# An expert's down projection in five products instead of six: features split 128 and 48, the 48 stacked as high and low parts

## The chip, the cores and the metric

One core of a Trainium2 chip runs the whole program. TensorE (PE) multiplies, VectorE (DVE) and ScalarE (ACT) do the elementwise work and move results out of PSUM, GpSimd (POOL) does some elementwise work and issues the indirect transfers, SyncE (SP) issues most of the others. The metric is the device time of one execution in microseconds (us).

## The reference, cut to what matters

The reference is one transformer block with modulation (adaLN): attention over 8 sequences of 256 tokens with 256 features, then a feed-forward part with one shared expert and 8 routed experts, two of which each token uses. Float32 inputs and outputs. The change touches only the routed experts:

```python
B, S, H, F, FS, N = (2, 128, 256, 176, 352, N_EXPERTS)      # here 2048 tokens, F = 176
g = jnp.einsum('th,nfh->ntf', h, gate_w)
u = jnp.einsum('th,nfh->ntf', h, up_w)
e = jnp.einsum('ntf,nhf->nth', jax.nn.silu(g) * u, down_w)   # the down projection: 176 -> 256
routed = jnp.einsum('nth,tn->th', e, wmat)
```

## The kernel before, in words

All products run on TensorE in the type `fp32r`, and each value is split into a high part (its rounding to that type) and a low part (the rest). `mm3` makes one product of three: low times high, high times low, high times high, lines 343, 344 and 345. Each matmul instruction is recorded with its weight load (PEld, LDWEIGHTS), of the stationary operand.

Attention, the shared expert and the routing run first, for 8 sequences interleaved by hand; the order on each engine is written out in the program, and engines meet at semaphores. The tokens are then scattered to a buffer sorted by expert, padded for each expert to tiles of 128 rows, and 39 tiles follow (`NT`). This is the routed stage. In step t the engines do, each in this order:

- TensorE: `pe_tile_up` of tile t+1 (six products with 352 moving columns: gate and up together), `pe_tile_act` of tile t (two transposes, line 1375, of the activated values `av` from rows to columns), `pe_tile_in` of tile t+3 (two transposes, line 1353), `pe_tile_down` of tile t-1 (six products with 256 moving columns).
- ScalarE: silu (line 1392), the high part of the activated values (`act_tile_act`, line 1396), the high part of the input (line 1388), the result of the down projection from PSUM to `yo` (line 1402).
- VectorE: silu times up (line 1430), the low part of the activated values (`dve_tile_lo`, line 1436), the low part of the input (line 1406), every fourth step four small operations on the routing data (lines 1419 to 1424), and in late steps one of the final additions (lines 1490 to 1502).
- GpSimd: the scatter of the finished rows (line 1441). SyncE: the loads of the tiles to come.

The down projection sums over 176 features. Before, they are cut into two halves of 88 (`FH`), both on partitions 0 to 87: two transposes of 88 columns, and two times three products with 88 rows each.

The weights of expert e come by two transfers (`sp_weights`) to one of two staging buffers `wstage`, ScalarE rounds them to the high part (`act_weights`), GpSimd or VectorE makes the low part (`split_weights`). Experts 0 and 1 are fetched at the start of the program, the others during attention, each when its buffer is free.

Of the kernel before, what the change touches and what calls it, by code (L numbers as in the profile page):

```python
# [8 lines left out]
ALU = mybir.AluOpType  # L9
ACT = mybir.ActivationFunctionType  # L10
F32 = mybir.dt.float32
# [5 lines left out]
ds = bass.ds  # L17

P = 128
# [9 lines left out]
def adaln_block(nc, x_in, w_qkv, b_cols, w_proj, b_proj, gate_col, cam_w0, cam_w1,  # L29
                router_t, gu_t, down_t, sh_gu_t, sh_down_t, c_t, w_mod, out):  # L30
    B, S, D = x_in.shape
    NE = router_t.shape[1]
    F = down_t.shape[1]
    FS = sh_down_t.shape[0]
    KD = D // P
# [3 lines left out]
    NT = (2 * T + NE * (P - 1)) // P  # L39
    REGION = T + P  # L40
    ROW = D + META
    FH = F // 2
    FT = [(f, min(P, FS - f)) for f in range(0, FS, P)]
    UNR = 3
    assert D == KD * P == 256 and S == TT * P == 256 and NT % UNR == 0 and F <= 256

    with ExitStack() as ctx:
        def sb(name, shape, dt=F32):
# [289 lines left out]
        def parts(t, *idx):  # L338
            return t[0][idx], t[1][idx]

        def mm3(pe, out_ap, l, r, start, stop):

            pe.matmul(out_ap, l[1], r[0], start=start, stop=False)  # L343
            pe.matmul(out_ap, l[0], r[1], start=False, stop=False)  # L344
            return pe.matmul(out_ap, l[0], r[0], start=False, stop=stop)  # L345
# [417 lines left out]
        if True:  # L763
# [71 lines left out]
            def sp_gate(sp, q):  # L835
                sp.dma_start(gring[q % 4][:], modrow[q:q + 1, 4 * D:5 * D].to_broadcast([P, D]).unsqueeze(1)).then_inc(gb_sems[q % 4], 16)

            def pool_setup(pool):
                pool.memset(minus_half[:], -0.5).then_inc(s_const, 1)
                pool.memset(eps_t[:], EPS).then_inc(s_const, 1)  # L840
                pool.memset(ident[:], 0.0).then_inc(s_const, 1)
                pool.memset(before[:], 0.0).then_inc(s_const, 1)
                pool.wait_ge(s_const, 4)
                pool.affine_select(out=ident[:], in_=ident[:], compare_op=ALU.not_equal, fill=1.0,
                                   base=0, pattern=[[-1, P]], channel_multiplier=1).then_inc(s_ident_ready, 1)

                pool.affine_select(out=before[:], in_=before[:], compare_op=ALU.is_ge, fill=1.0,
                                   base=0, pattern=[[-1, P]], channel_multiplier=1).then_inc(s_const, 1)
                pool.memset(ones[:], 1.0).then_inc(s_const, 1)
                pool.memset(ramp[:], 1.0).then_inc(s_const, 1)  # L850
                pool.iota(ebase[:], pattern=[[0, NB], [REGION // P, NE]], base=0, channel_multiplier=0,
                          allow_small_or_imprecise_dtypes=True).then_inc(s_const, 1)
                pool.wait_ge(s_const, 7)
                pool.affine_select(out=ramp[:], in_=ramp[:], compare_op=ALU.is_ge, fill=0.0,
                                   base=-NE, pattern=[[-NE, NR]], channel_multiplier=1).then_inc(s_const, 1)
                pool.iota(token_id[:], pattern=[[P, B * TT]], base=0, channel_multiplier=1,
                          allow_small_or_imprecise_dtypes=True).then_inc(s_const, 1)
                pool.iota(eidx[:], pattern=[[1, NE]], base=0, channel_multiplier=0,
                          allow_small_or_imprecise_dtypes=True).then_inc(s_const, 1)
                pool.iota(tidx[:], pattern=[[1, NT]], base=1, channel_multiplier=0,  # L860
                          allow_small_or_imprecise_dtypes=True).then_inc(s_const, 1)
                pool.iota(erow[:], pattern=[[REGION, NE]], base=0, channel_multiplier=0,
                          allow_small_or_imprecise_dtypes=True).then_inc(s_const, 1)
                for i, at, step in ((0, 0, 1), (1, 1, 1), (2, 0, REGION // P)):
                    pool.iota(pcols[:, i:i + 1], pattern=[[1, 1]], base=at, channel_multiplier=step,
                              allow_small_or_imprecise_dtypes=True).then_inc(s_const, 1)
                pool.memset(within[:, 0:1], 0.0).then_inc(s_const, 1)
                pool.wait_ge(s_const, 10 + 7)
# [370 lines left out]
            def pool_rstd1(pool, first, after):  # L1239
                at = slice(2 * TT * first, 2 * TT * after)  # L1240
                pool_rstd(pool, s_var1, after, mv1[:, at, 1], rs1[:, at], s_rstd1, 2 * first)
# [33 lines left out]
                sp.dma_start(mh[u][:], modrow[b:b + 1, 2 * D:4 * D].to_broadcast([P, 2 * D]).rearrange("p (j d) -> p j d", d=D)).then_inc((s_mh0_in, s_mh1_in)[u], 16)  # L1275

            eT = [tuple(h[:, 0, q * S:(q + 1) * S].rearrange("p (k n) -> p k n", k=KD) for h in h2T) for q in range(4)]
            avT = [tuple(h[0:FH, 1, q * S:(q + 1) * S].rearrange("p (k n) -> p k n", k=2) for h in h2T) for q in range(2)]

            sg = [wstage[q][:, 0:F] for q in range(2)]  # L1280
            av = [wstage[q][:, F:2 * F] for q in range(2)]
# [4 lines left out]
            xt_in = [h2all[:, r, :] for r in range(8)]  # L1286
            pad = exchange[:, 4 * ROW:5 * ROW]

            def expert(e, part, at, n):
                base = (0, W1, 2 * W1, 2 * W1 + W2)[part]  # L1290
                return experts_w[0:(P if part < 2 else FH), ds(e * WE + (base + at), n)]

            def bank2(t, n=256):
                return t[:, 0:2 * n].rearrange("p (a n) -> p a n", a=2)
# [4 lines left out]
            def sp_weights(sp, e, r):  # L1299

                if e >= 2:
                    sp.wait_ge((s_split_even, s_split_odd)[r], e // 2)
                sp.dma_start(wstage[r][:, 0:W1].rearrange("p (k n) -> p k n", k=KD),
                             gu_t[:, ds(e, 1), :].rearrange("(k p) o n -> p k (o n)", p=P)).then_inc((s_est0_in, s_est1_in)[r], 16)
                sp.dma_start(wstage[r][0:FH, W1:].rearrange("p (j n) -> p j n", j=2),
                             down_t[ds(e, 1)].rearrange("o (j p) n -> p (o j) n", p=FH)).then_inc((s_est0_in, s_est1_in)[r], 16)

            def act_weights(act, e):
                r = e % 2
                act.wait_ge((s_est0_in, s_est1_in)[r], 16 * (e - r) + 32)  # L1310
                if e == 0:
                    act.wait_ge(s_wlo_later, 2 + NF)
                    act.wait_ge(s_wlo, 3)
                    act.wait_ge(s_modrow_out, 16)
                    act.wait_ge(s_bvp_done, 1)
                elif e == NE // 2:
                    act.wait_ge(s_qk_done, 2 * B)
                elif e > NE // 2:
                    act.wait_ge(*((s_v_done, B), (s_v_done, B), (s_s2_done, B))[e - NE // 2 - 1])
                act.activation(expert(e, 0, 0, W1), wstage[r][:, 0:W1], ACT.Copy)  # L1320
                act.activation(expert(e, 2, 0, W2), wstage[r][0:FH, W1:], ACT.Copy).then_inc(s_ew_hi, 1)

            def split_weights(eng, e):
                r = e % 2
                eng.wait_ge(s_ew_hi, e + 1)
                eng.tensor_tensor(expert(e, 1, 0, W1), wstage[r][:, 0:W1], expert(e, 0, 0, W1).bitcast(F32), ALU.subtract)
                eng.tensor_tensor(expert(e, 3, 0, W2), wstage[r][0:FH, W1:], expert(e, 2, 0, W2).bitcast(F32),
                                  ALU.subtract).then_inc((s_split_even, s_split_odd)[r], 1)


# [40 lines left out]

            def pe_tile_act(pe, t, r):
                pe.wait_ge(s_ea_ready, t + 1)
                for j in range(2):
                    last = pe.transpose(ATb[r % 2][0:FH, j * P:(j + 1) * P], av[r % 2][:, j * FH:(j + 1) * FH], ident[:])  # L1375
                last.then_inc(s_eat_done, 1)

            def pe_tile_down(pe, experts, t, r):
                e = expert_of(pe, experts, r)
                pe.wait_ge(s_ea_lo, t + 1)  # L1380
                for j in range(2):
                    last = mm3(pe, EDN[r % 2][:, 0:D], parts(avT[r % 2], slice(None), j),
                               (expert(e, 2, j * D, D), expert(e, 3, j * D, D)), j == 0, j == 1)
                last.then_inc(s_edn_done, 1)

            def act_tile_in(act, t, r):
                act.wait_ge(s_ext_done, t + 1)
# [5 lines left out]

            def act_tile_act(act, t, r):
                act.wait_ge(s_eat_done, t + 1)
                act.activation(avT[r % 2][0], bank2(ATb[r % 2], P)[0:FH], ACT.Copy).then_inc(s_ea_hi, 1)

            def act_tile_out(act, t, r):
                act.wait_ge(s_edn_done, t + 1)
# [33 lines left out]
            def dve_tile_lo(dve, t, r):  # L1433
                q = r % 2
                dve.wait_ge(s_ea_hi, t + 1)
                dve.tensor_tensor(avT[q][1], bank2(ATb[q], P)[0:FH], avT[q][0].bitcast(F32), ALU.subtract).then_inc(s_ea_lo, 1)

            def pool_tile(pool, t):
                pool.wait_ge(s_emeta, META_OPS * (t // 4 + 1))
# [66 lines left out]
            with nc.Block() as block:  # L1506
# [68 lines left out]
                @block.gpsimd  # L1575
                def _(pool):
                    pool_setup(pool)
                    pool_rstd1(pool, 0, 1)
                    pool_rstd1(pool, 1, 2)
                    pool_rstd1(pool, 2, 4)  # L1580
# [675 lines left out]
```

## Time and profile before

| | |
|---|---|
| median of 3 runs | 291.94 us (290.74 to 292.01) |
| the profiled execution | 291.79 us, its span from the first to the last instruction 290.0 us |
| granted TensorE clock, mean | 0.976 of full speed |
| PE busy | 257.4 us, 89% of the span |
| DVE busy | 190.3 us, 66% |
| ACT busy | 161.2 us, 56% |
| POOL busy | 128.4 us, 44% |

The span is what the profile covers; the 1.8 us around it belong to the execution and not to any instruction. A busy share is an average over stages with different limits. A matmul's duration in the records is its way through the array, longer than the distance to the next one: what a stream of them costs is read from the distances between their starts.

### The profile page before, as it was taken

Reading aid. Unit: us, or ns where it says so; the run is one execution under the profiler, and the core shown is the slowest. Engines: PE = TensorE matmul, PEld = TensorE weight load, DVE = VectorE, ACT = ScalarE, POOL = GpSimd, SP = SyncE. Lnnn points to the kernel's source line nnn. Section 1 sums busy time; section 2 is a strip of 40 time slices with the busy share of each in tenths; the row PEclk is TensorE's granted clock in tenths of the full one; section 3 lists DMA queues with packets and bytes.
Section 4 is the critical chain, followed back from the end, with each engine's and each line's share of the span. In section 5 each row is a group of like instructions: output and inputs, shape, how many; then the busy total and the mean of one; then the engine's idle time right before and its main releaser. Section 6 shows DMA issues by size and latency. Waiting matters only on the chain.

```text
span 290.0 us, 6198 instructions
## 1 busy us (share of the span) xinstructions
PE 257.4 (89%) x1820; PEld 237.6 (82%) x1820; DVE 190.3 (66%) x579; ACT 161.2 (56%) x429; POOL 128.4 (44%) x146
## 2 busy tenths in 40 slices
PE   0899999898999999999999689999999999999900
PEld 0797688897889989888899579989999999999700
DVE  1675875139988581883697864745555467868893
ACT  2438568878467564747354554446566565656500
POOL 3120404654181078848972855203444454544630
PEclk9999999999999999999999999999999999999955
DMA  7894015341442013142320225344334485584464
GB/s 237 278 347 95 0 32 194 111 122 66 109 112 74 3 57 122 45 126 76 79 108 11 84 92 180 107 125 146 113 129 129 132 254 162 183 251 149 132 189 141
DMA packets 29319, 36.98 MB, mean 128 GB/s; under 512 B 4468, under 2 KB 23903, under 8 KB 29288
## 3 DMA queue, kind: packets, MB, share of 16 engines
q1 hardware_dynamic: 24056, 27.19, 32.3%
q0 software_dynamic: 3408, 8.46, 7.8%
q10 hardware_dynamic: 1824, 0.94, 1.1%
q8 instruction: 16, 0.26, 0.4%
q14 instruction: 15, 0.12, 0.2%
HBM read 24.78 MB, written 12.71 MB: 129 GB/s over the span
## 4 chain that ended last, share of the span: by engine, by line
PE 75%; DVE 7%; issue 5%; ACT 4%; DMA 3%; POOL 3%; ACTq 1%; SPq 0%; DVEq 0%; POOLq 0%
PE bank L343 17%; PE bank L345 17%; PE bank L344 16%; PE bank L1138 4%; PE bank L1353 3%; PE bank L1375 3%; PE bank L1110 3%; PE bank L1130 2%; PE bank L1093 2%; PE bank L1121 2%; PE bank L1102 2%; PE bank L1011 1%; DMA mh<-routed_out 1%; PE bank L540 1%; DMA routed_in<-h2all,slot_u 1%
## 5 line engine op out<-in xcount | busy, mean ns | idle before, releaser
L1441 POOL DMA_INDIRECT routed_out<-yo_all,dest x39 | 40.1, 1028 | 54.8 <-ACT yo_all L1402 35.5
L343 PE MATMUL bank<-experts_w,h2T_lo 128*128 (+1 forms) x156 | 50.6, 325 | 0.1
L345 PE MATMUL bank<-experts_w,h2T_hi 128*128 (+1 forms) x156 | 47.2, 303 | 0.0
L344 PE MATMUL bank<-experts_w,h2T_hi 128*128 (+1 forms) x156 | 47.0, 301 | 0.0
L706 POOL DMA_INDIRECT routed_in<-h2all,slot_u x32 | 31.5, 986 | 23.5 <-DVE slot_u L687 13.3
L1430 DVE SCALAR_TENSOR_TENSOR wstage<-wstage,wt,bank 128x176 f32<-128x176 f32 x39 | 15.5, 397 | 27.9 <-ACT wstage L1392 27.9
L343 PEld LDWEIGHTS bank<-experts_w,h2T_lo 128*128 128x128 f32 (+1 forms) x156 | 29.6, 190 | 0.5 <-issue 0.5
L344 PEld LDWEIGHTS bank<-experts_w,h2T_hi 128*128 128x128 f32 (+1 forms) x156 | 29.7, 190 | 0.0
L345 PEld LDWEIGHTS bank<-experts_w,h2T_hi 128*128 128x128 f32 (+1 forms) x156 | 29.4, 188 | 0.0
L343 PE MATMUL bank<-h2T_hi,wsgu_lo 128*128 128x256 f32 (+1 forms) x96 | 27.9, 290 | 1.5 <-issue 1.5
L345 PE MATMUL bank<-h2T_hi,wsgu_hi 128*128 128x256 f32 (+1 forms) x96 | 27.1, 282 | 1.1 <-issue 1.1
L344 PE MATMUL bank<-h2T_lo,wsgu_hi 128*128 128x256 f32 (+1 forms) x96 | 27.0, 281 | 0.0
L1392 ACT ACTIVATE wstage<-bank 128x176 f32<-128x176 f32 x39 | 12.4, 318 | 22.1 <-PE bank L345 22.1
L343 PE MATMUL bank<-hT_hi,wqk_lo 128*128 128x256 f32 x64 | 20.2, 316 | 2.0 <-DVE hT_lo L1223 2.0
L1402 ACT ACTIVATE yo_all<-bank 128x256 f32<-128x256 f32 x39 | 15.0, 385 | 11.8 <-PE bank L345 6.3
L1147 ACT ACTIVATE exchange<-bank,nm 128x256 f32<-128x256 f32 x32 | 14.8, 472 | 7.7 <-DVE nm L1208 6.1
L344 PE MATMUL bank<-hT_lo,wqk_hi 128*128 128x256 f32 x64 | 19.0, 297 | 0.0
L345 PE MATMUL bank<-hT_hi,wqk_hi 128*128 128x256 f32 x64 | 19.0, 297 | 0.0
L343 PEld LDWEIGHTS bank<-h2T_hi,wsgu_lo 128*128 128x128 f32 (+1 forms) x96 | 17.3, 180 | 2.0 <-issue 1.7
L345 PEld LDWEIGHTS bank<-h2T_hi,wsgu_hi 128*128 128x128 f32 (+1 forms) x96 | 17.3, 180 | 1.2 <-issue 1.2
L344 PEld LDWEIGHTS bank<-h2T_lo,wsgu_hi 128*128 128x128 f32 (+1 forms) x96 | 17.3, 180 | 0.1
L1208 DVE TENSOR_REDUCE nm<-bank 128x2 f32<-128x512 f32 x16 | 11.0, 689 | 8.7 <-PE bank L1093 5.4
(248 smaller groups left out, 760.6 us busy)
## 6 DMA issues: line engine op xcount, KB each, us to landing
h2all<-routed_in SPq DMA_DIRECT2D x39, 130.0 KB, 2.2
wstage<-gu_t SPq DMA_DIRECT2D x8, 352.0 KB
res<-x SPq DMA_DIRECT2D x4, 512.0 KB, 9.0
mx<-modrow SPq DMA_DIRECT2D x8, 256.0 KB, 3.7
mh<-modrow SPq DMA_DIRECT2D x8, 256.0 KB
exchange<-routed_out SPq DMA_DIRECT2D x8, 256.0 KB
wmod_s<-w_mod SPq DMA_DIRECT2D x3, 512.0 KB, 9.7
wstage<-down_t SPq DMA_DIRECT2D x8, 176.0 KB
```

The lines of the kernel that those rows point to most:

```text
L343: pe.matmul(out_ap, l[1], r[0], start=start, stop=False)
L344: pe.matmul(out_ap, l[0], r[1], start=False, stop=False)
L345: return pe.matmul(out_ap, l[0], r[0], start=False, stop=stop)
L706: pool.indirect_dma_start(out=routed_in, out_offset=bass.IndirectOffsetOnAxis(slot_u[:, i, j:j + 1], 0), in_=h2all[:, j % (2 * NB), :], in ...
L1110: last = pe.matmul(Sb[u][:, t * S:(t + 1) * S], th[u][:, t * P:(t + 1) * P], KL[u][:], start=False, stop=(t == TT - 1), skip_group_check=True)
L1138: last = pe.matmul(TR[u][:, t * D:(t + 1) * D], PT[u][:, k, t * P:(t + 1) * P], VV[u][:, k, P:P + D], start=(k == 0), stop=(k == TT - 1))
L1147: last = act.activation(pr[u][:, t, :], Sb[u][:, t * S:(t + 1) * S], ACT.Exp, bias=nm[u][:, i, t:t + 1], accum_out=ls[u][:, i, t:t + 1])
L1208: dve.tensor_reduce(nm[u][:, int(second), :], bank(Sb[u]), AX.X, ALU.max, negate=True).then_inc(s_max2 if second else s_max1, 1)
L1392: act.activation(sg[r % 2], EGU[r % 2][:, 0:F], ACT.Silu).then_inc(s_esilu, 1)
L1402: act.activation(yo[t % 6], EDN[r % 2][:, 0:D], ACT.Copy).then_inc(s_ey_ready, 1)
L1430: dve.scalar_tensor_tensor(av[q], sg[q], wt[:, t % 8:t % 8 + 1], EGU[q][:, F:2 * F], ALU.mult, ALU.mult).then_inc(s_ea_ready, 1)
L1441: pool.indirect_dma_start(out=routed_out, out_offset=bass.IndirectOffsetOnAxis(dest[:, t % 16:t % 16 + 1], 0), in_=yo[t % 6], in_offset=No ...
```

## The change

The 176 features of a tile are cut into 128 and 48 instead of 88 and 88. The first 128 take three products with 128 rows. The other 48 are handled in a block of 64 rows (`HALF`), features 112 to 175, in which the first 16 rows (`GAP`) meet zero weights. ScalarE copies the whole bank (its rows 64 to 127 of the second half hold nothing of use), and VectorE writes the low part of these 64 rows over partitions 64 to 127 of the high tile. The high weights of the 48 features are staged twice, in rows 16 to 63 and 80 to 127. Then one product of 128 rows gives high times high and low times high together, and one of 64 rows gives high times low: five in all. The second transpose has 64 columns of `av` instead of 88, the first 128. The staging buffers get two zeroed regions (`pool_stage_rows`), three transfers for the down weights of an expert instead of one, and the low part of a tile takes two VectorE instructions instead of one.

```diff
@@ -39,10 +39,12 @@
     NT = (2 * T + NE * (P - 1)) // P
     REGION = T + P
     ROW = D + META
-    FH = F // 2
+    HALF = P // 2
+    FB = F - P
+    GAP = HALF - FB
     FT = [(f, min(P, FS - f)) for f in range(0, FS, P)]
     UNR = 3
-    assert D == KD * P == 256 and S == TT * P == 256 and NT % UNR == 0 and F <= 256
+    assert D == KD * P == 256 and S == TT * P == 256 and NT % UNR == 0 and 0 < FB <= HALF
 
     with ExitStack() as ctx:
         def sb(name, shape, dt=F32):
@@ -835,6 +837,10 @@
             def sp_gate(sp, q):
                 sp.dma_start(gring[q % 4][:], modrow[q:q + 1, 4 * D:5 * D].to_broadcast([P, D]).unsqueeze(1)).then_inc(gb_sems[q % 4], 16)
 
+            def pool_stage_rows(pool):
+                for r in range(2):
+                    pool.memset(wstage[r][:, W1 + D:], 0.0).then_inc(s_const, 1)
+
             def pool_setup(pool):
                 pool.memset(minus_half[:], -0.5).then_inc(s_const, 1)
                 pool.memset(eps_t[:], EPS).then_inc(s_const, 1)
@@ -1275,7 +1281,7 @@
                 sp.dma_start(mh[u][:], modrow[b:b + 1, 2 * D:4 * D].to_broadcast([P, 2 * D]).rearrange("p (j d) -> p j d", d=D)).then_inc((s_mh0_in, s_mh1_in)[u], 16)
 
             eT = [tuple(h[:, 0, q * S:(q + 1) * S].rearrange("p (k n) -> p k n", k=KD) for h in h2T) for q in range(4)]
-            avT = [tuple(h[0:FH, 1, q * S:(q + 1) * S].rearrange("p (k n) -> p k n", k=2) for h in h2T) for q in range(2)]
+            avT = [tuple(h[:, 1, q * S:(q + 1) * S].rearrange("p (k n) -> p k n", k=2) for h in h2T) for q in range(2)]
 
             sg = [wstage[q][:, 0:F] for q in range(2)]
             av = [wstage[q][:, F:2 * F] for q in range(2)]
@@ -1286,9 +1292,9 @@
             xt_in = [h2all[:, r, :] for r in range(8)]
             pad = exchange[:, 4 * ROW:5 * ROW]
 
-            def expert(e, part, at, n):
+            def expert(e, part, at, n, rows=P):
                 base = (0, W1, 2 * W1, 2 * W1 + W2)[part]
-                return experts_w[0:(P if part < 2 else FH), ds(e * WE + (base + at), n)]
+                return experts_w[0:rows, ds(e * WE + (base + at), n)]
 
             def bank2(t, n=256):
                 return t[:, 0:2 * n].rearrange("p (a n) -> p a n", a=2)
@@ -1302,12 +1308,16 @@
                     sp.wait_ge((s_split_even, s_split_odd)[r], e // 2)
                 sp.dma_start(wstage[r][:, 0:W1].rearrange("p (k n) -> p k n", k=KD),
                              gu_t[:, ds(e, 1), :].rearrange("(k p) o n -> p k (o n)", p=P)).then_inc((s_est0_in, s_est1_in)[r], 16)
-                sp.dma_start(wstage[r][0:FH, W1:].rearrange("p (j n) -> p j n", j=2),
-                             down_t[ds(e, 1)].rearrange("o (j p) n -> p (o j) n", p=FH)).then_inc((s_est0_in, s_est1_in)[r], 16)
+                if e < 2:
+                    sp.wait_ge(s_const, 18 + e)
+                down = down_t[ds(e, 1)].rearrange("o f n -> f (o n)")
+                for to, of in ((wstage[r][:, W1:W1 + D], down[0:P]), (wstage[r][GAP:HALF, W1 + D:], down[P:F]),
+                               (wstage[r][HALF + GAP:P, W1 + D:], down[P:F])):
+                    sp.dma_start(to, of).then_inc((s_est0_in, s_est1_in)[r], 16)
 
             def act_weights(act, e):
                 r = e % 2
-                act.wait_ge((s_est0_in, s_est1_in)[r], 16 * (e - r) + 32)
+                act.wait_ge((s_est0_in, s_est1_in)[r], 64 * (e // 2 + 1))
                 if e == 0:
                     act.wait_ge(s_wlo_later, 2 + NF)
                     act.wait_ge(s_wlo, 3)
@@ -1318,13 +1328,13 @@
                 elif e > NE // 2:
                     act.wait_ge(*((s_v_done, B), (s_v_done, B), (s_s2_done, B))[e - NE // 2 - 1])
                 act.activation(expert(e, 0, 0, W1), wstage[r][:, 0:W1], ACT.Copy)
-                act.activation(expert(e, 2, 0, W2), wstage[r][0:FH, W1:], ACT.Copy).then_inc(s_ew_hi, 1)
+                act.activation(expert(e, 2, 0, W2), wstage[r][:, W1:], ACT.Copy).then_inc(s_ew_hi, 1)
 
             def split_weights(eng, e):
                 r = e % 2
                 eng.wait_ge(s_ew_hi, e + 1)
                 eng.tensor_tensor(expert(e, 1, 0, W1), wstage[r][:, 0:W1], expert(e, 0, 0, W1).bitcast(F32), ALU.subtract)
-                eng.tensor_tensor(expert(e, 3, 0, W2), wstage[r][0:FH, W1:], expert(e, 2, 0, W2).bitcast(F32),
+                eng.tensor_tensor(expert(e, 3, 0, W2), wstage[r][:, W1:], expert(e, 2, 0, W2).bitcast(F32),
                                   ALU.subtract).then_inc((s_split_even, s_split_odd)[r], 1)
 
 
@@ -1371,17 +1381,17 @@
 
             def pe_tile_act(pe, t, r):
                 pe.wait_ge(s_ea_ready, t + 1)
-                for j in range(2):
-                    last = pe.transpose(ATb[r % 2][0:FH, j * P:(j + 1) * P], av[r % 2][:, j * FH:(j + 1) * FH], ident[:])
+                pe.transpose(ATb[r % 2][:, 0:P], av[r % 2][:, 0:P], ident[:])
+                last = pe.transpose(ATb[r % 2][0:HALF, P:2 * P], av[r % 2][:, F - HALF:F], ident[:])
                 last.then_inc(s_eat_done, 1)
 
             def pe_tile_down(pe, experts, t, r):
                 e = expert_of(pe, experts, r)
                 pe.wait_ge(s_ea_lo, t + 1)
-                for j in range(2):
-                    last = mm3(pe, EDN[r % 2][:, 0:D], parts(avT[r % 2], slice(None), j),
-                               (expert(e, 2, j * D, D), expert(e, 3, j * D, D)), j == 0, j == 1)
-                last.then_inc(s_edn_done, 1)
+                to, (hi, lo) = EDN[r % 2][:, 0:D], avT[r % 2]
+                mm3(pe, to, (hi[:, 0], lo[:, 0]), (expert(e, 2, 0, D), expert(e, 3, 0, D)), True, False)
+                pe.matmul(to, hi[0:HALF, 1], expert(e, 3, D, D, HALF), start=False, stop=False)
+                pe.matmul(to, hi[:, 1], expert(e, 2, D, D), start=False, stop=True).then_inc(s_edn_done, 1)
 
             def act_tile_in(act, t, r):
                 act.wait_ge(s_ext_done, t + 1)
@@ -1393,7 +1403,7 @@
 
             def act_tile_act(act, t, r):
                 act.wait_ge(s_eat_done, t + 1)
-                act.activation(avT[r % 2][0], bank2(ATb[r % 2], P)[0:FH], ACT.Copy).then_inc(s_ea_hi, 1)
+                act.activation(avT[r % 2][0], bank2(ATb[r % 2], P), ACT.Copy).then_inc(s_ea_hi, 1)
 
             def act_tile_out(act, t, r):
                 act.wait_ge(s_edn_done, t + 1)
@@ -1433,7 +1443,9 @@
             def dve_tile_lo(dve, t, r):
                 q = r % 2
                 dve.wait_ge(s_ea_hi, t + 1)
-                dve.tensor_tensor(avT[q][1], bank2(ATb[q], P)[0:FH], avT[q][0].bitcast(F32), ALU.subtract).then_inc(s_ea_lo, 1)
+                hi, lo = avT[q]
+                dve.tensor_tensor(lo[:, 0], ATb[q][:, 0:P], hi[:, 0].bitcast(F32), ALU.subtract)
+                dve.tensor_tensor(hi[HALF:P, 1], ATb[q][0:HALF, P:2 * P], hi[0:HALF, 1].bitcast(F32), ALU.subtract).then_inc(s_ea_lo, 1)
 
             def pool_tile(pool, t):
                 pool.wait_ge(s_emeta, META_OPS * (t // 4 + 1))
@@ -1575,6 +1587,7 @@
                 @block.gpsimd
                 def _(pool):
                     pool_setup(pool)
+                    pool_stage_rows(pool)
                     pool_rstd1(pool, 0, 1)
                     pool_rstd1(pool, 1, 2)
                     pool_rstd1(pool, 2, 4)
```

## Rows read from the trace of the kernel before

**Rows 1.** The page: busy times of the engines, and the chain that ended last by engine.

```profile
PE 257.4 (89%) x1820; PEld 237.6 (82%) x1820; DVE 190.3 (66%) x579; ACT 161.2 (56%) x429; POOL 128.4 (44%) x146
...
PE 75%; DVE 7%; issue 5%; ACT 4%; DMA 3%; POOL 3%; ACTq 1%; SPq 0%; DVEq 0%; POOLq 0%
```

**Rows 2.** Busy times by stretch: its length, engines, granted clock, DMA share, GB/s.

```profile
225.00:250.00 25.00, 25.00 (x192) 24.54 (x191) 16.12 (x51) 14.99 (x48) 11.94 (x12) 1.00 0.59 180
```

**Rows 3.** A group by line and shape, 190 to 290 us: busy us, mean ns.

```profile
L344 PE MATMUL bank<-experts_w,h2T_hi 88*128 x78 | 22.0, 282 | 0.0
```

**Rows 4.** Timeline, one tile's period on PE: start, duration, engine, line, operands.

```profile
226.27 0.33 PE L343 MATMUL bank<-experts_w,h2T_lo 128*128 x1
...
227.58 0.36 PE L343 MATMUL bank<-experts_w,h2T_lo 88*128 x1
...
227.78 0.28 PE L344 MATMUL bank<-experts_w,h2T_hi 88*128 x1
...
227.90 0.28 PE L345 MATMUL bank<-experts_w,h2T_hi 88*128 x1
...
228.38 0.33 PE L343 MATMUL bank<-experts_w,h2T_lo 128*128 x1
```

**Rows 5.** Timeline, the low part and the product that needs it; VectorE late.

```profile
228.16 0.41 DVE L1436 TENSOR_TENSOR h2T_lo<-bank,h2T_hi 88x256 fp32r<-88x256 f32 x1
...
228.49 0.41 DVE L1406 TENSOR_TENSOR h2T_lo<-bank,h2T_hi 128x256 fp32r<-128x256 f32 x1
...
229.70 0.36 PE L343 MATMUL bank<-experts_w,h2T_lo 88*128 x1
...
244.75 0.40 DVE L1430 SCALAR_TENSOR_TENSOR wstage<-wstage,wt,bank 128x176 f32<-128x176 f32 x1 [0.45 <-ACT wstage L1392]
```

**Rows 6.** Timeline, leaving fp32r products with 8 stationary columns, with the weight load.

```profile
138.50 0.28 PE L345 MATMUL bank<-h2T_hi,wrt_hi 128*8 128x256 f32 x1
138.61 0.28 PE L343 MATMUL bank<-h2T_hi,wsgu_lo 128*128 128x256 f32 x1
...
138.50 0.19 PEld L343 LDWEIGHTS bank<-h2T_hi,wsgu_lo 128*128 128x128 f32 x1
```

**Rows 7.** Timeline around four transposes with 8 rows (plain fp32).

```profile
119.65 0.28 PE L345 MATMUL bank<-h2T_hi,wsgu_hi 128*128 128x256 f32 x1
119.86 0.41 PE L573 MATMUL bank<-ident,lg 8*128 8x8 f32 x4
...
119.86 0.32 PEld L573 LDWEIGHTS bank<-ident,lg 8*128 8x128 f32 x4
...
120.48 0.34 PE L344 MATMUL bank<-wv_lo,hT_hi 128*128 128x384 f32 x1
120.66 0.34 PE L345 MATMUL bank<-wv_hi,hT_hi 128*128 128x384 f32 x1
```

**Rows 8.** Timeline around four plain fp32 products, 8 stationary columns; two lines' durations (min/median/max).

```profile
31.10 0.34 PE L345 MATMUL bank<-wv_hi,hT_hi 128*128 128x384 f32 x1
31.37 1.88 PE L1011 MATMUL bank<-wmod_s,cS 128*8 128x512 f32 x4
...
33.46 0.34 PE L344 MATMUL bank<-wv_lo,hT_hi 128*128 128x384 f32 x1
...
L1011 PEld LDWEIGHTS bank<-wmod_s,cS x8: 85/90/90, 25.5 to 32.2; 128*8 128x8 f32 x8
L573 PE MATMUL bank<-ident,lg x16: 200/202/227, 95.0 to 162.4; 8*128 8x8 f32 x16
L1011 PE MATMUL bank<-wmod_s,cS x8: 592/592/597, 25.5 to 32.7; 128*8 128x512 f32 x8
```

**Rows 9.** The weights' transfers: issues on SP's queue, and POOL at the start.

```profile
L1305 SPq DMA_DIRECT2D wstage<-down_t x8: 420/421/1448, 15.1 to 142.1; - x8
...
39.52 0.30 SPq L832 DMA_DIRECT2D modrow<-mrow  x1
...
8.48 0.20 POOL L490 TENSOR_TENSOR rs<-mv,eps_t 128x4 f32<-128x4 f32 x1 [5.25 <-DVE mv L506]
```

## The prediction, made before the run

> **What bounds the kernel now.** I read the page first. Of the span of 290.0 us TensorE is busy 89%, VectorE 66%, and the chain that ended last lies on PE for 75% [rows 1]. The reader is to see that one engine sets the end; but a share is an average, so the stage of the change is read next. The table of stretches shows the routed stage with PE busy 25.00 of 25.00 us at the full granted clock (1.00), which is 2.4 GHz, VectorE at 16.12 and ScalarE at 14.99 [rows 2]. So PE alone sets the pace, and whatever a tile gains or loses on PE counts 39 times: the group of one down product has 78 members, two for each tile [rows 3].
>
> Then the timeline of one tile. The first up product starts at 226.27, and the same one of the next tile at 228.38: a period of 2.11 us [rows 4]. The six down products take 227.58 to 228.38, 0.80 us, and one starts 0.12 us after the other (227.78, 227.90). That distance is the price of a product, not the 0.28 us of its record, which overlaps the next. The first of the six has 0.20 us to its successor, since it follows a transpose; it stays.
>
> **The change part by part.**
>
> *Removed: one down product for each tile.* The new five have 256 moving columns as before, so each costs 0.12 us if nothing else changes: 39 x 0.12 = 4.7 us less.
>
> *The rows and columns used.* Four of the five products use 128 rows where 88 were used; up products with 128 rows stand in the same stream and show no more than their 352 columns. The fourth, high times low of the small block, has 64 rows and stands between two of 128, and the second transpose has 64 columns of its stationary side instead of 88. The question of this case is whether the array takes such a narrow instruction in its stride. No instruction here has 64 rows or columns; the nearest are those with 8.
>
> - Products of type fp32r with 8 stationary columns: the last starts at 138.50, the next wide one at 138.61, and the wide one's weight load starts at 138.50, under its predecessor [rows 6]. No cost at all.
> - Transposes with 8 rows: the product ahead starts at 119.65 and its place ends at 119.77; they start at 119.86, and so does the first of their weight loads, which is hidden no longer [rows 7]. Four of them take (0.41 - 0.20)/3 = 0.07 us each [rows 7, 8]. The product after next starts at 120.48; one distance of 0.18 us (120.66 - 120.48) before that, at 120.30, its predecessor really began. So the four filled 0.53 us where 0.28 would do: 0.25 us lost on the way in and out.
> - Plain fp32 products with 8 columns: from 31.10 + 0.18 = 31.28 to 33.46 - 0.18 = 33.28 are 2.00 us, for four at (1.88 - 0.59)/3 = 0.43 us, 1.72 [rows 8]. 0.28 us lost.
>
> The waits in front of these had been met long before, and the wide product of rows 6 has such waits and no gap; short duration isn't the cause either, since those of rows 8 are the longest of the kernel. What the two costly cases have in common is that the instruction uses a narrow part of the array, by rows or by columns, and that the weight loads are no longer hidden. The new product is fp32r, as the free case, but narrow by rows, as the 8-row case. I go by the rows: a cut by rows is nearer to a cut by rows than to one by columns.
>
> Its price then: the 0.28 us of rows 8, and in addition its own weight load of 128 columns, which takes 0.19 us where the 8-column one took 0.09 [rows 6, 8]: 0.28 + 0.10 = 0.38 us for each tile (estimate). Bounds: from below nothing [rows 6], or 0.25 if it behaves just as the 8-row ones; from above two loads at their full recorded 0.19 and two gaps of 0.09 (119.86 - 119.77), 0.56. I take 0.38. Net for each tile +0.38 - 0.12 = +0.26, and 39 x 0.26 = +10.1 us.
>
> The Trainium skill, page TensorEngine Tiling (Array Packing), section Tiling Modes, says that changing the tiling mode drains the engine, and counts 64 rows as a mode of its own; rows 7 and 8 agree with a drain, with 0.25 and 0.28 us. [...] The page TensorE: Matmul & The Clock Gate, section on LDWEIGHTS, gives a load as columns / 1.2 ns, 107 ns for 128; with two such loads exposed and the gap of 0.09 and one of 0.06 the estimate would be 0.36 us instead of 0.38.
>
> *The second transpose, 64 columns instead of 88.* It is narrow by columns and fp32. By rows 6 it costs nothing, by rows 8 0.28 us more. The first is fp32r and the second isn't a transpose, so neither settles it; I take nothing, since the transposes of the tile are handled like the fp32r stream around them (no gap between them and it), and keep 0.28 as a rival.
>
> *The low part in two VectorE instructions.* They have 128 columns each, as many elements per partition in all as before. One with 88 and one with 128 partitions take the same 0.41 us, and the next starts after 0.33 [rows 5]. So the additional one costs VectorE between nothing and 0.33 us. The product that needs it starts at 229.70, the low part ends at 228.57: 1.13 us of cover. Behind it on VectorE waits the low part of the next input, and then silu times up, ahead of which 0.45 us are idle even in a late step with a final addition [rows 5]. With a period that grows by 0.26 the cover grows too. Nothing. Were it gone (period shorter by 0.12, and the full 0.33), the 0.45 would be used up and PE would wait for its transposes. ScalarE's copy gets more partitions, not more elements on each: nothing, by the same two VectorE rows.
>
> *The weights.* 16 more issues on SP at 0.42 us [rows 9]. Those for experts 0 and 1 begin at 15.1, and what follows them on SP goes out at 39.52, when its data are there [rows 9]. The others delay the rows of modulation behind them by 0.84 us each, which are fetched ahead of use; bounds 0 to 0.8 us, I take 0. SP's new wait for the zeroed regions stands ahead of the transfers at 15.13 and later, while POOL has 5.25 us idle before 8.48 [rows 9], room for two memsets. The copy and split of the weights keep their 512 elements for each partition.
>
> **Sum.** -4.7 + 14.8 (39 x 0.38) = +10.1 us. The profiled execution is 291.79 us, span 290.0; it becomes 301.9 with a span of 300.1. Its time is 0.15 below the median of 291.94, so the forecast for the median is 302.0 us.
>
> **The rivals.**
>
> *The 64-row product costs nothing extra* (as rows 6). Period 1.99 us, 39 x 0.12 = 4.7 us gained: 287.2 us. For it: same type, same stream as the free case. Against it: it is the rows that are cut. It ends on the other side; it holds if the loss at the narrow product is under 0.12 us, and the sign turns there.
>
> *The transpose pays too.* 0.28 us more for each tile, 10.9 us: 302.0 + 10.9 = 312.9 us. For it: rows 8. Against it: the columns are cut in a transpose, which none of the costly cases is.
>
> *Only the transpose pays.* -0.12 + 0.28 = +0.16, 6.2 us: 298.2 us.
>
> *VectorE takes over,* beside the first rival only: some 0.3 us in each of 14 late steps with a final addition, at most 4 us, which would eat the gain: 287.2 to 291.
>
> **How the numbers follow.** My forecast 0.52; no cost at the narrow product 0.22; both pay 0.18; only the transpose 0.05; VectorE or late weights eat the gain 0.03. The forecast's own range is 297.0 (0.25 us at the product, +5.1 us) to 304.5 (0.44, between 0.38 and the upper bound). The whole range has to take in the first rival and leaves out the case in which both pay: 286.8 to 304.5 us. A measurement of this kernel tells some 0.5%, 1.5 us, from no change; within it lies next to nothing: 0.03. Faster 0.23, slower 0.74.
>
> **What the profile after would show.** If I am right: 64-row products in a group of 39; the weight load of that product and that of its successor start after their predecessor's place has ended, not under it; the period is 2.37 us; PE still counts as busy throughout. If the first rival holds, the load of the 64-row product starts with the product ahead of it and the period is 1.99. If the transposes pay, the loads of the second one of line 1375 and of the first of line 1353 start late. Idle time of PE ahead of a down product with VectorE's line 1447 or so as its releaser would say that the two low parts are the bound. The prediction is wrong above all if a cut by rows is treated like rows 6; then all of the +14.8 falls away.

## The result, and the profile after

The changed kernel takes 300.71 us (median of 4 runs, 299.33 to 302.16) beside 291.98 us: 1.029 times the time before, 95% interval 1.021 to 1.037. With more runs on another chip, below, it is 1.034 (1.029 to 1.038). It is slower by 3%, as forecast (302.0 us). The profiled execution took 302.16 us with a span of 300.3 us; the forecast for it was 301.9 and 300.1.

The page of the kernel after, busy times and chain, beside [rows 1]:

```profile
PE 267.9 (89%) x1781; PEld 238.5 (79%) x1781; DVE 199.6 (66%) x618; ACT 161.4 (54%) x429; POOL 128.6 (43%) x148
...
PE 75%; DVE 8%; issue 5%; ACT 4%; DMA 3%; POOL 2%; ACTq 1%; SPq 0%; DVEq 0%
```

TensorE executes 39 instructions fewer (1781 instead of 1820), and is busy 10.5 us longer. VectorE has 39 instructions and 9.3 us more; the chain is the same within a point for each engine. The stretch in the middle of the routed stage, as in [rows 2]:

```profile
225.00:250.00 25.00, 25.00 (x161) 21.97 (x159) 15.35 (x54) 13.35 (x43) 10.31 (x11) 1.00 0.50 151
```

PE is still busy for 25.00 of 25.00 us at the full granted clock, with 161 instructions where 192 were done. The column to look at is the second: weight loads are under way for 21.97 us instead of 24.54. In a stream in which each load lies under its predecessor this shouldn't fall; the 128-row version below shows 24.73. The timeline of one tile on PE and the loads to its down products, beside [rows 4]:

```profile
229.06 0.33 PE L345 MATMUL bank<-experts_w,h2T_lo 128*128 x1
...
230.37 0.36 PE L345 MATMUL bank<-experts_w,h2T_lo 128*128 x1
230.57 0.28 PE L346 MATMUL bank<-experts_w,h2T_hi 128*128 x1
230.69 0.28 PE L347 MATMUL bank<-experts_w,h2T_hi 128*128 x1
230.90 0.38 PE L1393 MATMUL bank<-experts_w,h2T_hi 64*128 x1
231.21 0.38 PE L1394 MATMUL bank<-experts_w,h2T_hi 128*128 x1
231.43 0.33 PE L345 MATMUL bank<-experts_w,h2T_lo 128*128 x1
...
233.82 0.33 PE L345 MATMUL bank<-experts_w,h2T_lo 128*128 x1
```

```profile
230.57 0.19 PEld L347 LDWEIGHTS bank<-experts_w,h2T_hi 128*128 128x128 f32 x1
230.90 0.18 PEld L1393 LDWEIGHTS bank<-experts_w,h2T_hi 64*128 64x128 f32 x1
231.21 0.19 PEld L1394 LDWEIGHTS bank<-experts_w,h2T_hi 128*128 128x128 f32 x1
231.31 0.19 PEld L345 LDWEIGHTS bank<-experts_w,h2T_lo 128*128 128x128 f32 x1
```

Lines 345 to 347 are `mm3`, line 1393 is the 64-row product, line 1394 the last one. The load for line 347 starts at 230.57, with the product ahead of it; the product itself starts 0.12 us later. The load for the 64-row product should start at 230.69 by that pattern. It starts at 230.90, after the place of line 347 has ended (230.81) and 0.09 us more. The load for line 1394 doesn't start with the 64-row product either, but 0.31 us after it. From 230.69 to 231.43 there are 0.74 us for three products of 0.12 us: 0.38 us lost. The period is 2.37 us (229.06 to 231.43) and 2.39 us (231.43 to 233.82) instead of 2.11.

And what didn't happen, a gap at the transposes ahead of these products:

```profile
230.02 0.27 PE L1384 MATMUL bank<-ident,wstage 128*128 128x128 f32 x1
230.12 0.27 PE L1385 MATMUL bank<-ident,wstage 128*64 128x128 f32 x1
230.23 0.38 PE L1363 MATMUL bank<-ident,h2all 128*128 128x128 f32 x2
```

The one with 64 columns (line 1385) starts 0.10 us after the wide one and is followed after 0.11 us: no gap on either side.

### The profile page after: what moved, and what is told of

It reads as the page before. It is cut to its first block, busy times and chain, and to the rows that moved or that the text cites. A ratio compares the mean times of both kernels' runs of the same rounds, so it can differ in the third digit from the quotient of the medians.

```text
span 300.3 us, 6176 instructions
## 1 busy us (share of the span) xinstructions
PE 267.9 (89%) x1781; PEld 238.5 (79%) x1781; DVE 199.6 (66%) x618; ACT 161.4 (54%) x429; POOL 128.6 (43%) x148
## 4 chain that ended last, share of the span: by engine, by line
PE 75%; DVE 8%; issue 5%; ACT 4%; DMA 3%; POOL 2%; ACTq 1%; SPq 0%; DVEq 0%
PE bank L345 15%; PE bank L347 14%; PE bank L346 14%; PE bank L1394 4%; PE bank L1393 4%; PE bank L1144 3%; PE bank L1363 3%; PE bank L1116 2%; PE bank L1136 2%; PE bank L1099 2%; PE bank L1127 2%; PE bank L1108 2%; PE bank L1384 1%; PE bank L1385 1%; PE bank L1017 1%
## 5 line engine op out<-in xcount | busy, mean ns | idle before, releaser
L345 PE MATMUL bank<-experts_w,h2T_lo 128*128 x117 | 39.7, 339 | 0.1
L347 PE MATMUL bank<-experts_w,h2T_hi 128*128 x117 | 36.1, 309 | 0.0
L346 PE MATMUL bank<-experts_w,h2T_hi 128*128 x117 | 36.1, 308 | 0.0
L345 PEld LDWEIGHTS bank<-experts_w,h2T_lo 128*128 128x128 f32 x117 | 22.1, 189 | 0.5 <-issue 0.5
L346 PEld LDWEIGHTS bank<-experts_w,h2T_hi 128*128 128x128 f32 x117 | 22.3, 190 | 0.0
L347 PEld LDWEIGHTS bank<-experts_w,h2T_hi 128*128 128x128 f32 x117 | 22.0, 188 | 0.0
L1416 DVE TENSOR_TENSOR h2T_lo<-bank,h2T_hi 128x256 fp32r<-128x256 f32 x39 | 16.6, 425 | 2.4 <-ACT h2T_hi L1398 1.2
```

The source lines that it names most:

```text
L1416: dve.tensor_tensor(eT[r][1], bank2(XTb[r % 2], P), eT[r][0].bitcast(F32), ALU.subtract).then_inc(s_ex_lo, 1)
```

## The experiments

Theory: a product that is narrow by rows costs 0.38 us, on its way in and out, whatever else is around it, and the rest of the change is hidden. Rivals: the cost lies in the stacking, in the second low-part instruction or in the transfers; or each narrow product costs by itself; or it is a matter of the accumulation in PSUM. Every run was timed beside the kernel before on its own chip; ratios compare across chips, times do not.

### All 128 rows in the fourth product

```diff
-                pe.matmul(to, hi[0:HALF, 1], expert(e, 3, D, D, HALF), start=False, stop=False)
+                pe.matmul(to, hi[:, 1], expert(e, 3, D, D), start=False, stop=False)
```

> The changed kernel, but its fourth down product takes all 128 rows of both sides instead of 64 (the rows below add low times low, which is nothing or a gain in precision). Theory (a narrow-by-rows product costs 0.38 us on its way in and out, all else is hidden): the loss is gone, every product starts 0.12 us after the one before, period 1.99 us, time 39 x 0.12 = 4.7 us under the kernel before, 287.2 us. Rival 1 (the second low-part instruction or the product of stacked parts is what costs): nothing changes, 301 us. Rival 2 (the narrow product costs, but VectorE or the weights' transfers eat the gain): 289 to 292 us, with PE idle ahead of a down product or of the transposes.

Measured: 286.80 us beside 290.76, ratio 0.984 (0.979 to 0.989), so 4.7 us less by the ratio. The down products in its timeline:

```profile
230.02 0.28 PE L347 MATMUL bank<-experts_w,h2T_hi 128*128 x1
230.14 0.28 PE L1393 MATMUL bank<-experts_w,h2T_hi 128*128 x1
230.26 0.28 PE L1394 MATMUL bank<-experts_w,h2T_hi 128*128 x1
230.38 0.33 PE L345 MATMUL bank<-experts_w,h2T_lo 128*128 x1
...
232.37 0.33 PE L345 MATMUL bank<-experts_w,h2T_lo 128*128 x1
```

0.12 us from each to the next, period 1.99 us. The loads fill the stretch again (second column):

```profile
225.00:250.00 25.00, 25.00 (x191) 24.73 (x190) 20.38 (x67) 15.68 (x51) 13.09 (x13) 1.00 0.66 200
```

Between this kernel and the changed one lies only the height of one product, 128 rows instead of 64 on both of its sides, and the five products give what they promised. This is the version to keep: it is 1.6% under the kernel before (1.1 to 2.1), and as it adds low times low, it leaves out less of the sum. Both rivals of the expectation are out: the stacking and the second low part are in this kernel and cost no gap, and PE never waits in this stretch for VectorE or the transfers.

### The kernel before, with one product cut to 64 rows

```diff
-                for j in range(2):
-                    last = mm3(pe, EDN[r % 2][:, 0:D], parts(avT[r % 2], slice(None), j),
-                               (expert(e, 2, j * D, D), expert(e, 3, j * D, D)), j == 0, j == 1)
-                last.then_inc(s_edn_done, 1)
+                to, (hi, lo) = EDN[r % 2][:, 0:D], avT[r % 2]
+                mm3(pe, to, (hi[:, 0], lo[:, 0]), (expert(e, 2, 0, D), expert(e, 3, 0, D)), True, False)
+                pe.matmul(to, lo[:, 1], expert(e, 2, D, D), start=False, stop=False)
+                pe.matmul(to, hi[0:64, 1], expert(e, 3, D, D)[0:64], start=False, stop=False)
+                pe.matmul(to, hi[:, 1], expert(e, 2, D, D), start=False, stop=True).then_inc(s_edn_done, 1)
```

> The kernel before, six products, 88 and 88 features, one transfer, one low-part instruction; only one of the six products for each tile is cut from 88 to 64 rows (24 of the 176 features lose their high times low part). Theory: 39 x 0.38 = 14.8 us more, 306.8 us, period 2.49 us, the weight load of the narrow product and of its successor late. Rival 1 (not the width but the stacking, the second low-part instruction or the transfers): 292 us, period 2.11.

Measured: 305.42 us beside 290.76, ratio 1.051 (1.046 to 1.056): 14.7 us for 39 narrow products, 0.376 us each. Its timeline shows the same three distances as that of the changed kernel:

```profile
231.87 0.28 PE L1383 MATMUL bank<-experts_w,h2T_lo 88*128 x1
232.08 0.38 PE L1384 MATMUL bank<-experts_w,h2T_hi 64*128 x1
232.39 0.39 PE L1385 MATMUL bank<-experts_w,h2T_hi 88*128 x1
232.61 0.33 PE L343 MATMUL bank<-experts_w,h2T_lo 128*128 x1
```

Nothing of the change is in this kernel but the width of one product, and less work costs 5%. The price is measured by itself.

### 96 rows, and 32

```diff
-                pe.matmul(to, hi[0:HALF, 1], expert(e, 3, D, D, HALF), start=False, stop=False)
+                pe.matmul(to, hi[0:96, 1], expert(e, 3, D, D, 96), start=False, stop=False)
```

> The changed kernel with 96 rows in its fourth product instead of 64 (32 of the rows below come in, low times low). Theory (what counts is whether the instruction fits in half of the array's rows): as with 128 rows, 287.2 us, period 1.99. Rival (any product with fewer rows than its neighbours pays, in proportion or in full): between 290 and 301 us, a gap ahead of the 96-row product.

Measured: 286.79 us beside 290.76, ratio 0.987 (0.981 to 0.992). The 96-row product has no gap on either side:

```profile
231.12 0.28 PE L347 MATMUL bank<-experts_w,h2T_hi 128*128 x1
231.24 0.28 PE L1393 MATMUL bank<-experts_w,h2T_hi 96*128 x1
231.36 0.29 PE L1394 MATMUL bank<-experts_w,h2T_hi 128*128 x1
```

To be narrower than one's neighbours costs nothing at 96 rows. The trace of the kernel before could have told that, though the prediction looked only at the instructions with 8 rows or columns: the shared expert's down products go from 128 to 96 rows, each 0.12 us after the one ahead, and the 88-row products of the routed stage are followed by a 128-row one as closely (228.26 to 228.38).

```profile
190.46 0.28 PE L345 MATMUL bank<-wsd_hi,aT_hi 128*128 128x256 f32 x1
190.58 0.28 PE L343 MATMUL bank<-wsd_hi,aT_lo 96*128 96x256 f32 x1
190.70 0.28 PE L344 MATMUL bank<-wsd_lo,aT_hi 96*128 96x256 f32 x1
```

The other kernel is the same edit with `hi[0:32, 1]` and 32 rows of the weights.

> The changed kernel with 32 rows in its fourth product instead of 64 (half of the high times low part of the 48 features is left out). Theory (the change of width costs, not the width): the same 0.38 us, period 2.38, 300.7 us. Rival (cost grows as the product gets narrower, or a quarter of the rows is cheaper to load): more than 1.5 us away from 300.7.

Measured: 298.56 us beside 288.87, ratio 1.034 (1.030 to 1.039). The distances are those of 64 rows:

```profile
231.81 0.29 PE L347 MATMUL bank<-experts_w,h2T_hi 128*128 x1
232.03 0.38 PE L1393 MATMUL bank<-experts_w,h2T_hi 32*128 x1
232.33 0.39 PE L1394 MATMUL bank<-experts_w,h2T_hi 128*128 x1
232.56 0.33 PE L345 MATMUL bank<-experts_w,h2T_lo 128*128 x1
```

### Two narrow products, together and apart

```diff
                 mm3(pe, to, (hi[:, 0], lo[:, 0]), (expert(e, 2, 0, D), expert(e, 3, 0, D)), True, False)
                 pe.matmul(to, hi[0:HALF, 1], expert(e, 3, D, D, HALF), start=False, stop=False)
+                pe.matmul(to, hi[0:HALF, 1], expert(e, 3, D, D, HALF), start=False, stop=False)
```

> The changed kernel with its 64-row product issued twice in a row (that part of the sum is counted twice). Theory (the cost is that of the change from wide to narrow and back): only 0.12 us more for each tile, since the second narrow one has its weight load under the first: period 2.50 us, 39 x 0.12 = 4.7 us over the changed kernel, 305.4 us. Rival (each narrow product costs by itself, because its own load is never hidden): 0.31 us or more for each tile, the distance from its start to the next in the changed kernel, 12 us, 313 us or more.

Measured: 305.20 us beside 290.76, ratio 1.051 (1.046 to 1.056).

```profile
230.10 0.28 PE L347 MATMUL bank<-experts_w,h2T_hi 128*128 x1
230.31 0.38 PE L1393 MATMUL bank<-experts_w,h2T_hi 64*128 x1
230.53 0.28 PE L1394 MATMUL bank<-experts_w,h2T_hi 64*128 x1
230.74 0.38 PE L1395 MATMUL bank<-experts_w,h2T_hi 128*128 x1
230.97 0.33 PE L345 MATMUL bank<-experts_w,h2T_lo 128*128 x1
```

From 230.10 to 230.97 are 0.87 us for four products of 0.12: 0.39 us lost, as with one. So the second of two in a row costs no more than any other product. In the next tile the record of the first starts at 232.82, and the load of the second 0.11 us later, under the first:

```profile
232.93 0.19 PEld L1394 LDWEIGHTS bank<-experts_w,h2T_hi 64*128 64x128 f32 x1
```

The two have the same operands; a pair with different ones was not run. Now the two apart:

```diff
-                mm3(pe, to, (hi[:, 0], lo[:, 0]), (expert(e, 2, 0, D), expert(e, 3, 0, D)), True, False)
+                pe.matmul(to, lo[:, 0], expert(e, 2, 0, D), start=True, stop=False)
+                pe.matmul(to, hi[0:HALF, 1], expert(e, 3, D, D, HALF), start=False, stop=False)
+                pe.matmul(to, hi[:, 0], expert(e, 3, 0, D), start=False, stop=False)
+                pe.matmul(to, hi[:, 0], expert(e, 2, 0, D), start=False, stop=False)
```

> The changed kernel with the 64-row product issued twice as in the run with two together, but one of them between the first and the second of the three wide products, so that there are two changes to narrow and two back (that part of the sum is counted twice). Theory (the cost is that of the change): 0.38 + 0.12 = 0.50 us for each tile over the changed kernel, period 2.88 us, 320 us. Rival (the cost is that of the number of narrow products or of the six instructions): 305 us, as with two together.

Measured: 317.29 us beside 288.87, ratio 1.100 (1.095 to 1.105). The same six instructions as in the kernel before this one, in another order, and 4.9% of the kernel before more: some 14 us, 0.36 us for each tile.

```profile
232.37 0.38 PE L1393 MATMUL bank<-experts_w,h2T_hi 64*128 x1
232.68 0.39 PE L1394 MATMUL bank<-experts_w,h2T_hi 128*128 x1
232.90 0.28 PE L1395 MATMUL bank<-experts_w,h2T_hi 128*128 x1
233.11 0.38 PE L1396 MATMUL bank<-experts_w,h2T_hi 64*128 x1
233.42 0.39 PE L1397 MATMUL bank<-experts_w,h2T_hi 128*128 x1
```

Each return to width is 0.31 us behind the narrow one. The pair of runs settles it: what is paid for is the way into narrow products and out, not the number of them.

### The narrow product first

```diff
-                mm3(pe, to, (hi[:, 0], lo[:, 0]), (expert(e, 2, 0, D), expert(e, 3, 0, D)), True, False)
-                pe.matmul(to, hi[0:HALF, 1], expert(e, 3, D, D, HALF), start=False, stop=False)
+                pe.matmul(to, hi[0:HALF, 1], expert(e, 3, D, D, HALF), start=True, stop=False)
+                mm3(pe, to, (hi[:, 0], lo[:, 0]), (expert(e, 2, 0, D), expert(e, 3, 0, D)), False, False)
```

> The changed kernel with its 64-row product first of the five, right behind the transposes. Theory (the way in and the way out are paid wherever it stands): 0.38 us for each tile as in the changed kernel, period 2.38 us, 300.7 us. Rival (what costs is an accumulation in PSUM that goes from wide to narrow to wide within one sum): some 0.2 us less for each tile, 293 us.

Measured: 298.72 us beside 288.87, ratio 1.034 (1.030 to 1.039), the same as in its old place.

```profile
231.98 0.18 PEld L1392 LDWEIGHTS bank<-experts_w,h2T_hi 64*128 64x128 f32 x1 [0.17 <-issue]
```

```profile
231.99 0.38 PE L1392 MATMUL bank<-experts_w,h2T_hi 64*128 x1
232.29 0.38 PE L345 MATMUL bank<-experts_w,h2T_lo 128*128 x1
```

The load path is idle for 0.17 us before the narrow load, right behind the transposes, and the way back to width takes 0.30 us as before. No sum in PSUM goes from wide to narrow here, so that turn within a sum, the rival's condition, isn't the cause.

### The side work, without the new products

The kernel before with the side work of the change: two low-part instructions of 128 columns, three transfers for the down weights, the memsets and the wait. It has neither the new transposes nor the write to partitions 64 to 127; these are in the 128-row version.

```diff
+                for p0, p1 in ((0, 48), (48, 68), (68, FH)):
+                    sp.dma_start(wstage[r][p0:p1, W1:].rearrange("p (j n) -> p j n", j=2),
...
+                dve.tensor_tensor(avT[q][1][:, 0], ATb[q][0:FH, 0:P], avT[q][0][:, 0].bitcast(F32), ALU.subtract)
+                dve.tensor_tensor(avT[q][1][:, 1], ATb[q][0:FH, P:2 * P], avT[q][0][:, 1].bitcast(F32), ALU.subtract).then_inc(s_ea_lo, 1)
```

> The kernel before with everything of the change but the products: the low part in two VectorE instructions of 128 columns, the down weights of an expert in three transfers, the two memsets at the start and SP's wait for them. Theory (all of that is hidden): no change, 290.8 us beside 290.8, within 0.5%, period 2.11 us. Rival (a part of the measured loss, or of the missing gain of the 128-row version, lies here): 1 us or more slower.

Measured: 288.22 us beside 288.87, ratio 0.997 (0.995 to 1.000). No loss, and if anything a gain of 0.3% that I don't explain. So the rival of a loss here is out by a second way. The memsets take 0.56 us from 3.28 on, in time in which GpSimd still waits 4.50 us:

```profile
3.28 0.56 POOL L840 MEMSET wstage<- 128x256 f32 x2
8.34 0.20 POOL L490 TENSOR_TENSOR rs<-mv,eps_t 128x4 f32<-128x4 f32 x1 [4.50 <-DVE mv L506]
```

### The changed kernel again, and the second low part

> The changed kernel once more, with more runs, since the first interval (2.1% to 3.7% slower) is wide. Theory (39 x 0.26 us): 1.035 of the kernel before, with an interval that holds 1.034. Rival (a part of the 0.26 us is given back elsewhere, for instance behind the last tile): 1.029 or less.

Measured: 298.23 us beside 288.73, ratio 1.034 (1.029 to 1.038). The forecast of 1.035 lies inside; the first, wider interval held it too. The forecast's ratio, 302.0 to 291.94, is 1.034 too. The first middle of 1.029 lies inside the scatter of its four runs.

The timeline of VectorE after showed one thing more than expected, so the last run moved the target of the second low-part instruction, in the version with 128 rows:

```diff
-                dve.tensor_tensor(hi[HALF:P, 1], ATb[q][0:HALF, P:2 * P], hi[0:HALF, 1].bitcast(F32), ALU.subtract).then_inc(s_ea_lo, 1)
+                dve.tensor_tensor(lo[0:HALF, 1], ATb[q][0:HALF, P:2 * P], hi[0:HALF, 1].bitcast(F32), ALU.subtract).then_inc(s_ea_lo, 1)
```

> The version with 128 rows in all products, but the second low-part instruction of VectorE writes to the partitions it reads from (0 to 63 of the low tile) instead of 64 to 127 of the high tile; the sum then leaves out low times high of the 48 features. In the changed kernel the two low-part instructions take 0.30 and 0.32 us from start to start where two unshifted ones take 0.20. Theory A (writing to other partitions than it reads costs the overlap with its neighbours): 0.20 us each here. Theory B (128 partitions instead of 88, or the instruction ahead, costs it): 0.30 here as well. Either way the time stays within 0.5% of the 128-row version, since VectorE is hidden.

The edit leaves out more than this says. Partitions 64 to 127 of the high tile now keep what ScalarE copied there, and two products of 128 rows count it in: this kernel serves for its times alone, its sums are not those of the reference.

VectorE in the 128-row version, and here:

```profile
226.30 0.28 DVE L1447 TENSOR_TENSOR h2T_lo<-bank,h2T_hi 128x128 fp32r<-128x128 f32 x1
226.59 0.28 DVE L1448 TENSOR_TENSOR h2T_hi<-bank,h2T_hi 64x128 fp32r<-64x128 f32 x1
226.91 0.42 DVE L1416 TENSOR_TENSOR h2T_lo<-bank,h2T_hi 128x256 fp32r<-128x256 f32 x1
```

```profile
226.06 0.28 DVE L1447 TENSOR_TENSOR h2T_lo<-bank,h2T_hi 128x128 fp32r<-128x128 f32 x1
226.26 0.27 DVE L1448 TENSOR_TENSOR h2T_lo<-bank,h2T_hi 64x128 fp32r<-64x128 f32 x1
226.46 0.41 DVE L1416 TENSOR_TENSOR h2T_lo<-bank,h2T_hi 128x256 fp32r<-128x256 f32 x1
```

Shifted, the instruction starts 0.29 us after the one ahead of it, when the record of that one has ended (226.58), and the next starts 0.32 us later, when its own has (226.87); unshifted, 0.20 and 0.20, each before its predecessor's record has ended. The durations are nearly the same (0.28 beside 0.27 us). Theory B is out: 128 partitions and the instruction ahead are in both kernels. Theory A fits, but the edit changed two more things with the shift: the output goes to another tile, `hi`, from which the instruction also reads, and it starts on another partition than the output of the instruction ahead. Which of the three costs the overlap was not separated. The ratio is 0.988 (0.982 to 0.994), beside 0.984 (0.979 to 0.989) of the shifted version: no difference of the time is seen, since VectorE is hidden.

## Why the prediction was right

**The pace.** PE alone sets it, before and after: 25.00 of 25.00 us busy in both. So each change to a tile's PE time counted 39 times, in both directions: 0.376 x 39 up in the kernel with one product cut, 0.12 x 39 down in the one with five wide ones.

**The removed product.** Forecast -4.7 us; the 128-row version gives 4.7 by its ratio (3.3 to 6.0 by its interval).

**The way in and out of the narrow product.** Forecast 0.38 us (bounds 0 and 0.56); measured 0.38 in the timeline of the changed kernel and 0.376 by the time of the kernel before with one product cut. The choice that decided the sign was to go by the 8-row transposes and not by the free 8-column products, though the latter had the right type. It was a choice by likeness: no row of before showed an fp32r product with few rows, and the rival had 0.22. That it fell on the right side is in part luck. That both ways are paid once for two narrow products together and twice for two apart is shown. The Trainium skill, page TensorEngine Tiling (Array Packing), section Tiling Modes, says that a change of tiling mode drains the engine. The runs agree in so far as the change is what costs; no trace shows a mode of the engine, only loads that start late.

The size came out of the 8-column plain products (0.28) and 0.10 for the longer load of its own. The parts can be read now: 0.21 us instead of 0.12 ahead of it (0.09), 0.31 behind it (0.19 more) and 0.22 behind the first wide one (0.10 more), 0.38 in all. Read with the loads, these are two gaps of 0.09 us and two loads of 0.10 us that lie under no product: the load of line 345 starts at 231.31, 0.10 us after that of line 1394. So the size was right by its parts too. The second, lower estimate of 0.36 us took 0.06 for the gap on the way out, a number that no row beside it gives; it measured 0.09.

**The second transpose.** Taken at nothing, kept as a rival at 0.28 us: no gap at its 64 columns. That rival would have given 312.9 us. Its chance of 0.18 wasn't ruled out by anything in the trace of before; why 8 plain fp32 columns pay and 64 transposed ones don't is still open.

**VectorE.** Costed at nothing within bounds of 0 and 0.33 us for each tile. The bound was almost reached: low part to next input takes 0.61 us (226.30 to 226.91) where one instruction took 0.33 [rows 5], 0.28 us more. Cover was there. In the 128-row version, with its shorter period, VectorE is busy for 20.38 of 25.00 us in the stretch of [rows 2] where it was 16.12; in part this is because six final additions fall into it instead of four. In its steps with a final addition nothing is left of the 0.45 us that VectorE was idle ahead of silu times up, yet PE stays busy for 25.00 of 25.00 us. So the fourth rival (VectorE takes over) came near, and still didn't come.

**Weights and memsets.** Taken at nothing; with the side work in the kernel before, 0.997.

**The first rival** (no cost at the narrow product, 287.2 us) is what the 128-row version does. The prediction named the point at which the sign turns, a loss of 0.12 us; the loss was three times that.

## What to carry to other kernels

Before you count products, look at their shapes: an fp32r product with 64 or 32 rows between wide ones costs 0.38 us here, three products' worth, and filling it up to 96 or 128 rows, as was done here with low parts, costs nothing. Where narrow products are needed, issue them in a row, so that the way in and out is paid once. A gap of this kind hides in a PE that counts as busy all the time: look for a weight load that starts after its predecessor's place instead of under it, and for a falling share of the loads in a stretch (21.97 of 25.00 us beside 24.54).

## What the runs showed of the hardware that wasn't expected

- The loss is a step, not a slope: 128, 96 and 88 rows cost nothing, 64 and 32 rows the same 0.38 us. The step lies between 64 and 88 rows.
- It depends on rows and columns in different ways: fp32r products with 8 stationary columns [rows 6] and a transpose with 64 are free, plain fp32 products with 8 columns are not [rows 8].
- The VectorE instruction that reads partitions 0 to 63 and writes 64 to 127 of the high tile loses the overlap with both neighbours, 0.09 us ahead and 0.12 behind, though its own record is hardly longer (0.28 beside 0.27 us). Whether it is the shift, the start partition after that of the instruction ahead, or the tile was not separated.
